# Two GpSimd gathers of a graph network: a wait at each turn of the ring for the last group's transfers

## What is computed

```python
# x: (6250, 256), edges src -> dst, sorted by dst; 16 edge types
def gnn0(x):                      # L0
    deg   = zeros(16, N).at[etype, dst].add(1); deg = maximum(deg, 1)
    h_all = einsum('nd,rdo->rno', x, W_r)                       # a table of 16 rows per node
    msg   = h_all[etype, src] / deg[etype, dst][:, None]        # first gather
    return segment_sum(msg, dst) + x @ W0.T + b

def gnn1(x):                      # L1
    h    = x @ W
    norm = dinv[src] * dinv[dst]                                # with self loops
    return leaky_relu(segment_sum(norm[:, None] * h[src], dst) + b, 0.2)   # second gather

x = x + gnn0(layernorm(x))
x = x + moe(layernorm(x))
x = x + gnn1(layernorm(x))
x = x + lstm_head(layernorm(x))
```

## Time and profile before

| | us |
|---|---|
| three timed runs, median | 4071.44 (4070.2 to 4076.07) |
| span of the profiled execution | 4443.8 |
| first gather, from its first issue to its last add | 1211.0 |
| second gather, the same | 1171.9 |

### The profile page before, as it was taken

How to read it: one execution, slowest core, us unless ns; L and a number is a source line. 1 busy time by engine, 2 the same in 40 slices (tenths; PEclk the granted TensorE clock), 3 DMA queues, 4 the chain that set the end, 5 groups by cost and what they waited for, 6 DMA issues and landing times. The chain is left out here.

```text
span 4443.8 us, 59668 instructions
## 1 busy us (share of the span) xinstructions
PE 3422.0 (77%) x18753; PEld 2613.4 (59%) x18753; DVE 1898.4 (43%) x5881; ACT 912.0 (21%) x2407; POOL 1686.3 (38%) x1769
## 2 busy tenths in 40 slices
PE   7999999455567666667999554566667779999996
PEld 3444444354556555565666444445555557999996
DVE  4555300133334444454555421223334445544687
ACT  2333333000000111112333200000000002444554
POOL 1000000566666666653222366666666660000000
PEclk9999999677777777778999766777888889999998
DMA  4333444333444545553333323333444444433333
GB/s 148 149 149 149 154 168 164 116 107 110 124 122 144 161 134 148 150 150 108 116 113 110 109 86 94 107 116 122 126 138 146 152 154 147 153 126 119 110 109 113
DMA packets 246926, 580.34 MB, mean 131 GB/s; under 512 B 45059, under 2 KB 130588, under 8 KB 232783
## 3 DMA queue, kind: packets, MB, share of 16 engines
q1 hardware_dynamic: 158816, 334.44, 21.9%
q0 software_dynamic: 85344, 238.92, 18.3%
q10 hardware_dynamic: 2448, 3.15, 0.2%
HBM read 384.29 MB, written 191.42 MB: 130 GB/s over the span
## 5 line engine op out<-in xcount | busy, mean ns | idle before, releaser
L1676 POOL DMA_INDIRECT b_msg<-scratch_gx,k_src_row x782 | 770.6, 985 | 385.2 <-issue 220.0
L941 POOL DMA_INDIRECT a_msg<-scratch_hrel,k_rel_row x782 | 755.1, 966 | 424.1 <-issue 214.8
L717 PE MATMUL r_psm<-k_w,r_xnT 128*128 128x512 f32 x1568 | 696.4, 599 | 10.4 <-ACT k_slab L681 9.5
L1019 PE MATMUL a_ps<-a_hit,a_msg 128*128 128x128 f32 x3128 | 556.5, 343 | 170.6 <-issue 112.9
L1727 PE MATMUL b_ps<-b_hit,b_msg 128*128 128x128 f32 x3128 | 481.2, 317 | 197.3 <-issue 117.9
L1019 PEld LDWEIGHTS a_ps<-a_hit,a_msg 128*128 128x128 f32 x3128 | 501.3, 248 | 209.6 <-issue 137.4
L1727 PEld LDWEIGHTS b_ps<-b_hit,b_msg 128*128 128x128 f32 x3128 | 462.8, 230 | 246.4 <-issue 148.4
L2130 PE MATMUL l_psg<-k_hall,k_whhT 128*128 128x125 f32 x4640 | 550.7, 277 | 5.2 <-DVE k_hall L2256 5.2
L2130 PEld LDWEIGHTS l_psg<-k_hall,k_whhT 128*128 128x128 f32 x4640 | 538.4, 193 | 5.7 <-DVE k_hall L2256 5.7
L717 PEld LDWEIGHTS r_psm<-k_w,r_xnT 128*128 128x128 f32 x1568 | 294.2, 192 | 356.0 <-issue 342.5
L1831 DVE TENSOR_TENSOR k_accT<-k_accT,b_ps 128x256 f32 x196 | 82.6, 422 | 654.2 <-remote 476.0
(11 more groups left out here) (290 smaller groups left out, 4200.4 us busy)
## 6 DMA issues: line engine op xcount, KB each, us to landing
l_xr<-scratch_xrow SPq DMA_DIRECT2D x146, 512.0 KB
scratch_hrel<-k_slab SPq DMA_DIRECT2D x50, 1024.0 KB
scratch_hrel<-r_hst SPq DMA_DIRECT2D x48, 1024.0 KB
scratch_xrow<-n_xs SPq DMA_DIRECT2D x50, 512.0 KB
a_typ<-scratch_typ SPq DMA_DIRECT2D x196, 96.0 KB
a_msg<-scratch_hrel,k_rel_row POOLq DMA_INDIRECT x782
b_msg<-scratch_gx,k_src_row POOLq DMA_INDIRECT x782
n_xb<-scratch_gx SPq DMA_DIRECT2D x48, 256.0 KB
```

Source lines behind the costliest of these rows:

```text
L717: mm = pe.matmul(psm[:, c % 4], xnT[:, u, kk], k.w[:, kk, c * 512:(c + 1) * 512], start=(kk == 0), stop=(kk == 1))
L941: pool.indirect_dma_start(msg[:, q, j], None, table, bass.IndirectOffsetOnAxis(ap=rows_of[:, g, j:j + 1].bitcast(U32), axis=0)).then_inc(s ...
L1019: mm = pe.matmul(ps[:, u, kk, 0:WIN], msg[:, g % SL, j, kk * P:(kk + 1) * P], hit[:, u, j], start=(j == 0), stop=(j == pieces(g)[-1]))
L1676: pool.indirect_dma_start(msg[:, q, j], None, rows_of, bass.IndirectOffsetOnAxis(ap=k.src_row[:, g, j:j + 1].bitcast(U32), axis=0)).then_i ...
```

## The change

In both gather loops, when group g is the first of a new turn of the ring (q == 0, not the first time), GpSimd waits behind `hold` until the transfers of group g - 1, in the ring's last place, have landed:

```diff
@@ stage_first, tiles, gpsimd
                             if g >= SL:
                                 hold(k, pool, s_mm, g - SL + 1)
+                            if q == 0 and g >= SL:
+                                for j in pieces(g - 1):
+                                    pool.wait_ge(s_m[SL - 1][j], 16 * (g // SL))
                             for j in pieces(g):
                                 pool.indirect_dma_start(
```

## The result

| | median of the runs, us | lowest to highest | profiled span, us |
|---|---|---|---|
| before | 4073.8 (4 runs) | 4070.2 to 4076.1 | 4443.8 |
| changed | 4220.0 (4 runs) | 4213.9 to 4222.5 | 4220.7 |

The ratio is 1.0357, with a 95% interval of 1.0343 to 1.0372: 146 us slower. The direction and the places were as forecast, and so was the kind of cost. The size was not: 103 us were predicted, and the time lies 24 us above the range's upper end. The profiled span went the wrong way too. It fell by 223 us, where 0 to 60 us of growth were expected.

The account below looks back on a forecast made before the run. The prediction took GpSimd's issue rate to bound both gathers. Each turn was to cost 1.50 + 0.75 - 0.30 = 1.95 us, over 53 turns 103 us: 4071.4 + 103 = 4175 us, range 4100 to 4196.

Parts of the forecast that it names:

- The bound: Both gathers, unprofiled, run at GpSimd's own issue rate with nearly no slack: 782 x 1.258 = 984 us each.
- The sum of 4097: Whole kernel before: stretches without gathers 2060.9, two gathers of 984, tails 34.1 and 24.1, one wait 10.3 us.
- The price of a turn: At every seventh group of each gather, GpSimd's pause was to cost 1.95 us, over 53 turns 103 us.
- the first term: At a turn, the time from the last issue's end to its transfer's landing, put at 1.50 us.
- The "high" bound of 4.0 us: Upper bound of a turn, from the x_xr load's 4.5 us issue to landing: 212 us over 53 turns.
- The free first turn: The second gather's first turn costs nothing, since GpSimd waits over 10 us for TensorE there, leaving 53 turns.
- The profiled span should grow by ... 0 to 60 us: Whole profile: growth of 0 to 60 us, because 321 us of slack swallow part of the pauses.
- the slack: GpSimd's waits for TensorE in the gathers: 321 us in the profile, at most 103 in the timed runs.
- Absorbed: In the gathers, TensorE sets the pace and pauses shorten GpSimd's waits: 4071 us or part of the cost; chance 0.12.
- Faster by a forced drain: In mid-burst turns of the gathers, draining GpSimd's queue frees VectorE and TensorE earlier: 50 us gain, 4020; chance 0.06.
- The wait that does nothing: At the turns, the last group has already landed, so time stays at 4071 us; chance 0.02.
- gaps over 3 us at the turns: In the changed kernel's profile, such GpSimd gaps would put the cost above the range; about 2.2 us was expected.

Follow-up runs that it names:

- second recording: The kernel before, unedited, profiled once more: one run of 4069.8 us, its profiled span 4068.0 us.
- 2: Against the kernel before, the change's wait in the first gather alone: 4147.5 us, ratio 1.0185.
- experiment 3: Against the kernel before, the same four waits at each turn, but on transfers of the group before the last: 4071.8 us, ratio 1.0001.
- 5: Against the kernel before, a wait at each turn for three of the last four transfers, not the youngest: 4152.9 us, ratio 1.0193.
- 6: Against the kernel before, two turns with the wait in each round of the ring instead of one: 4363.0 us, ratio 1.0705.
- experiment 8: Against the kernel before, every group's fourth piece not fetched, TensorE multiplying the third's rows twice: 3649.5 us, ratio 0.8953.
- experiment 7: Against the kernel before, the ring of seven groups held to four, with no wait on transfers: 4086.9 us, ratio 1.0028.
- disturbed recording: The first profile of the unedited kernel before: span 4443.8 us.
- experiments 9 and 10: Unused 2 x 256 KB sync-engine loads at every seventh group of the second gather: with the change's waits 4242.0 us, in the kernel before 4073.2 us.
- experiment 4: Against the kernel before, four waits at every group from the third on, for transfers of the group before the last: 4079.3 us, ratio 1.0013.

## Why the prediction was right in kind and too low

**The bound.** Right. The prediction took the timed program to be bound by GpSimd's issue rate, by subtracting the stretches without gathers from the timed median. The second recording shows that, and of the experiments that tested it 2, 3, 5, 6 and 8 came out as it says; 7 is 4 us outside.

The sum of 4097 that stood for it was 29 us too high, and not because a step is 1.242 us: the step is 1.258. The tails of 34.1 and 24.1 us and the wait of 10.3 were taken from the disturbed recording. In the second one the tails are 8.5 and 5.6 us (1798.5 to 1807.0 and 3317.2 to 3322.8) and there is no such wait, while the issues take 995.1 and 1001.4 us in place of 984 each. The sentence that TensorE doesn't lack gathered data does not hold for the undisturbed program: there 257 of the 265 us of idle time before its matmuls of the first gather end with a landing.

**The price of a turn.** Three terms were added: 1.50 + 0.75 - 0.30 = 1.95 us. Two hold: from landing to the next issue the changed kernel's turns show 0.79 and 0.78 us, and the usual gap is 0.305.

**The failed step is the first term, "from the end of the last issue to the landing ... 1.50 us".** In the changed kernel its mean is 2.48 us in the first gather and 2.11 in the second (medians 2.28 and 1.84). There were two errors in it:
- The number was read from the last packet in the queue, and packets are not the landing. At the 54 turns the landing comes 0.38 us on average (0.29 to 0.84) after the end of the queue's last packet. The quickest landing at a turn is 1.73 us after its issue's end, 0.23 later than the 1.50. In the quiet turn shown above it is 1.88 us after it, at 1263.03, while the last packet of GpSimd's queue ends at 1262.66.
- It was read from a single pause in which the queue had the DMA engines to itself. That is the floor and not the mean. In 20 of the 54 turns the sync queue moved under 40 KB from the start of the last issue to the next issue, and their mean is 2.69 us; in the other 34 it is 3.32. The first gather has more of such traffic than the second, and the higher mean. That other traffic prolongs a turn is shown by experiments 9 and 10; that it accounts for all of the difference between turns is not, since the correlation over the 54 is 0.63. One turn of the second gather took 3.98 us with no packet on the sync queue; a 16 KB packet of an instruction queue (q8), which took 1.45 us, fell into it. Whether that packet caused the delay wasn't tested.

The prediction held both a floor and a mean to be one number, and put its own tolerance at 1.5 to 2.3 us a turn. The "high" bound of 4.0 us was set aside because that row is another shape. What was measured (2.97 and 2.59 us, net) lies between the two. With the right term the sum is 27 x (2.48 + 0.79 - 0.305) + 27 x (2.11 + 0.78 - 0.305) = 150 us. Of the 47 us between 103 and 150 this term makes 43 (54 x 0.80); the rest is the 54th turn and 0.04 us of restart at each.

Where the time of a landing goes can be read at the turns, because GpSimd's queue is empty after each pause. The first packet of the next transfer starts 1.66 us after its issue's start at the median of the 54 (1.65 at least), so 0.7 us after the instruction's end. In the quiet turn the last transfer's packets run from 1.70 to 2.50 us after its issue's start and it lands at 2.87.

The Trainium skill, "DMA: Bandwidth & Descriptors", in its section on the anatomy of one DMA on the gpsimd path, gives the formula that came to an estimated 2.3 us for 128 KB. These transfers never reach it: the landings that the changed kernel's trace has, 418 of 782 in each gather, take 2.7 us at least, 2.8 to 3.0 at the median, 7.6 at the most. The same section of the Trainium skill puts most of the fixed cost on the write's receipt. The trace doesn't agree: the larger part lies before the first packet (1.66 us), and 0.38 us after the last one. That section of the Trainium skill also says that the semaphore is only raised when the last byte is confirmed landed. That whoever waits is exposed to the whole landing is the prediction's own conclusion from it, and the 54 pauses bear it out.

**The free first turn.** Wrong, though small. The prediction let the first turn of the second gather cost nothing because GpSimd waited 10.55 us for TensorE just there. In the second recording TensorE is done in time (the gap there is 0.30 us), and in the changed kernel the turn's pause is 2.87 us like any other. The long wait at that place was part of the disturbed recording; a ring of four meets one there in an undisturbed run too (experiment 7).

**"The profiled span should grow by ... 0 to 60 us".** Wrong, and for a reason that was at hand. The prediction had found that the slack could not be in the timed runs, but then took it for an effect that every recording has. It belonged to that one recording. In each of the other eleven the recorded execution is one of the timed ones, and its span is 1.7 to 2.2 us below its time. Why TensorE's releases were held back in the first (in both gathers, with the other stretches untouched) stays open. TensorE's granted clock was lower there, 0.73 and 0.78 against 0.81 and 0.85 in the second recording; whether as a cause or because TensorE did less at a time, nothing here shows.

**The rivals.** Absorbed: ruled out by the second recording and experiment 8. Faster by a forced drain: it needed held-back releases, and there are none; four waits without a pause change nothing (experiment 3). The wait that does nothing: the 54 pauses are there. The sign given by the prediction for a cost above its range, gaps over 3 us at the turns, is what came: the first gather's mean is 3.27.

No version here that fetches all rows beats the kernel before. What bounds it, 782 issues of 1.258 us for each gather, is what would have to be made fewer or shorter; no run here tried it.

## What to carry to other kernels

When the profiled span and the timed runs are 9% apart, record again before reading any wait, or count only what the timed runs have room for. A wait of an issuing engine for its own youngest transfer cost the rest of the landing plus the restart at every turn here; for a transfer one group older it cost nothing here. So wait for the older one wherever that is enough. And take a latency for a sum from its distribution over the stretch concerned, with the traffic that is there: the value of one quiet moment is the floor.

## What the runs showed of the hardware

- An indirect DMA of 128 rows (128 KB) occupies GpSimd for 0.953 us, and the next one starts 0.305 us later whether or not it has waits on things that are already there (experiments 1, 3 and 4). After a true wait it takes 0.78 us from landing to issue.
- Such a transfer lands 2.6 to 2.7 us after its issue's start at best (1.66 us to its first packet, some 0.8 us of packets, some 0.4 us from the last packet to the landing), and in the changed kernel 7.6 us after it at the slowest, while the sync queue moved 1.8 MB; 512 KB beside it cost a waiting engine about 1 us (3.85 against 2.89).
- TensorE's granted clock, a mean over its levels of 1.2 and 2.4 GHz, was 0.79 in the first gather of the changed kernel, 0.81 in that of before (second recording) and 0.88 with three of four pieces fetched. The same instructions made 721.6, 699.4 and 634.9 us of busy time there. In the slower kernel the engine waited more and was granted less. It didn't show in the time: GpSimd's own issues account for 80 of the 81.3 us by which the first gather grew.
- Four semaphore waits that are already met cost GpSimd 0.01 us at most (experiment 4).
